# Convolution stage of a mixed convolution and attention block: gram runs joined, subtractions moved and reordered

## What is computed

```python
def _L0_conv_ref(feature, conv_w, conv_b):          # K = 7, PAD = 3
    norm = jnp.sqrt(jnp.sum(feature * feature, axis=1, keepdims=True))
    feat_n = feature / jnp.maximum(norm, EPS)
    feat_pad = jnp.pad(feat_n, ((0, 0), (0, 0), (PAD, PAD), (PAD, PAD)))
    corr = jnp.stack([jnp.sum(feat_pad[:, :, r:h + r, cc:w + cc] * feat_n, axis=1)
                      for r, cc in _offsets()], axis=1)
    x = jnp.concatenate([feature, corr], axis=1)
    return jnp.einsum('bchw,oc->bohw', x, conv_w) + conv_b[None, :, None, None]
...
x = x + _L0_conv_ref(_gn(x), L0_conv_conv_w, L0_conv_conv_b)      # _gn: group norm, 32 groups
t = _to_tokens(x)
t = t + _L1_attn_ref(_ln_t(t), ...)
t = t + _L1_ffn_ref(_ln_t(t), ...)
```

## Time and profile before

| | us |
|---|---|
| median of three runs | 2792.21 (2791.79 to 2792.80) |
| the profiled execution | 2792.42 |
| its span, first to last instruction | 2790.6 |

### The profile page before, as it was taken

How to read it: one execution, slowest core, us unless ns; L and a number is a source line. 1 busy time by engine, 2 the same in 40 slices (tenths; PEclk the granted TensorE clock), 3 DMA queues, 4 the chain that set the end, 5 groups by cost and what they waited for, 6 DMA issues and landing times. The chain is left out here.

```text
span 2790.6 us, 59188 instructions
## 1 busy us (share of the span) xinstructions
PE 2578.2 (92%) x23728; PEld 1255.5 (45%) x23728; DVE 1854.0 (66%) x2383; ACT 1543.3 (55%) x2626; POOL 1420.2 (51%) x1113
## 2 busy tenths in 40 slices
PE   4888568999999999999999999999499999999999
PEld 3555233454544444444544544533144444444444
DVE  6887258888898888888888887785333333333332
ACT  2334035667666676676666666666344444444443
POOL 2333155778778778787778776777210101111010
PEclk8889778999999999999999999999799999999999
DMA  3121232113113112112131121110300101010110
GB/s 139 64 95 56 102 90 69 35 37 106 37 32 102 42 32 99 32 41 90 32 105 36 39 77 45 32 47 2 113 23 23 46 23 45 23 45 23 28 40 23
DMA packets 67442, 151.45 MB, mean 54 GB/s; under 512 B 13313, under 2 KB 17342, under 8 KB 67198
## 3 DMA queue, kind: packets, MB, share of 16 engines
q1 hardware_dynamic: 67198, 148.05, 16.7%
HBM read 59.17 MB, written 37.75 MB: 35 GB/s over the span
## 5 line engine op out<-in xcount | busy, mean ns | idle before, releaser
L1377 POOL TENSOR_TENSOR b_pair<-b_ex 128x512 f32<-128x512 f32 x768 | 975.0, 1296 | 341.7 <-ACT b_ex L1249 341.6
L1249 ACT ACTIVATE b_ex<-b_st 128x512 f32<-128x512 f32 x1536 | 870.1, 598 | 408.1 <-PE b_st L911 372.6
L1084 DVE TENSOR_REDUCE b_mxp<-b_mx 128x4 f32<-128x2048 f32 x384 | 877.8, 2286 | 153.2 <-PE b_mx L927 152.2
L911 PE MATMUL b_st<-b_qst,b_kst 97*128 97x256 f16 (+1 forms) x3072 | 548.5, 277 | 22.0 <-ACT b_ex L1249 8.5
L1633 DVE TENSOR_TENSOR c_gs<-c_g,c_gs 128x512 f16<-128x512 f32 x192 | 132.8, 692 | 482.2 <-ACT c_gs L1706 482.2
L1554 PE MATMUL c_hid<-c_z,c_wi 128*128 128x512 f16 x1728 | 406.3, 381 | 11.3 <-DVE c_z L1626 11.3
L944 PE MATMUL b_pv<-b_ex,b_v 128*32 128x256 f32 x6144 | 411.9, 386 | 1.9 <-ACT b_pvs L1257 1.7
L1569 PE MATMUL c_acc<-c_gs,c_wo 128*128 128x512 f16 x1728 | 404.0, 379 | 0.0
L911 PEld LDWEIGHTS b_st<-b_qst,b_kst 97*128 97x128 f16 (+1 forms) x3072 | 216.0, 97 | 370.6 <-ACT b_ex L1249 201.2
L1702 ACT ACTIVATE c_g<-c_hid,c_bias 128x512 f32<-128x512 f32 x192 | 131.4, 684 | 363.3 <-PE c_hid L1554 363.1
L1554 PEld LDWEIGHTS c_hid<-c_z,c_wi 128*128 128x128 f16 x1728 | 169.5, 98 | 228.3 <-issue 20.2
(11 more groups left out here) (169 smaller groups left out, 2715.5 us busy)
## 6 DMA issues: line engine op xcount, KB each, us to landing
a_x<-in_x SPq DMA_DIRECT2D x8, 1536.0 KB, 9.3
after_conv<-a_x SPq DMA_DIRECT2D x24, 512.0 KB, 2.6
b_xl<-after_conv SPq DMA_DIRECT2D x8, 1536.0 KB, 8.8
b_qst<-b_staged0q SPq DMA_DIRECT2D x192, 64.0 KB, 2.0
b_kst<-b_staged0k SPq DMA_DIRECT2D x192, 64.0 KB, 2.0
b_v<-b_vstaged SPq DMA_DIRECT2D x24, 512.0 KB, 2.9
b_xr<-after_conv SPq DMA_DIRECT2D x8, 1536.0 KB, 6.4
after_attention<-b_xr SPq DMA_DIRECT2D x8, 1536.0 KB, 5.4
```

The source lines that it names most:

```text
L911: last = nc.tensor.matmul(st[n % NST][:, j * QUERIES:(j + 1) * QUERIES], kst[g][0:depth, s, kt * P:(kt + 1) * P], qst[g][0:depth, s, q0:q0 ...
L1084: nc.vector.reduce_max(mxp[x % 2][:, w // 2, :, w % 2], mx[:, :, :], AX_X).then_inc(mx_taken, 1)
L1249: nc.scalar.activation(ex[u % 2][e][s][:, :], st[n % NST][:, :], ACT.Exp, scale=SCALE).then_inc(exp_ready, 1)
L1377: nc.gpsimd.tensor_tensor(pair[u % 2][s][:, :], ex[u % 2][0][s][:, :], ex[u % 2][1][s][:, :], ALU.add).then_inc(pair_ready, 1)
```

## The change

TensorE runs both gram halves in one piece, then sums of squares, then means. VectorE's list is put in another order: masks of half 0, low correlations of image s - 1 (which were the last thing in the step of that image), statistics, masks of half 1, `within_groups`, inverse norms, evictions with unit features. The low halves of the unit features go to GpSimd, at the head of its step, behind a wait for both gram halves of image s. Every instruction that is computed stays the same; only its place changes, and for the low halves the engine.

```diff
                     correlate(0)
+                    correlate(1)
                 if real(s + 1):
                     squared_norms(s + 1)
-                if real(s):
-                    correlate(1)
...
-            def unit_features(i, p, n):
-
-                if n < KC:
-                    dve.wait_ge(clamped, INVERSE * (2 * i + 2))
-                    nc.vector.tensor_tensor(sq[:, n, :], f[p][:, n, :], nrm[:, :], ALU.mult
-                                            ).then_inc(fn_ready, 1)
-                else:
-                    k = n - KC
-                    dve.wait_ge(fn_ready, KC * i + k + 1)
-                    dve.wait_ge(fnhi_ready, KC * i + k + 1)
-                    nc.vector.tensor_tensor(fn[1][:, k, 0:NPIX], sq[:, k, :], fn[0][:, k, 0:NPIX],
-                                            ALU.subtract).then_inc(fnlo_ready, 1)
+            def unit_features(i, p, k):
+                dve.wait_ge(clamped, INVERSE * (2 * i + 2))
+                nc.vector.tensor_tensor(sq[:, k, :], f[p][:, k, :], nrm[:, :], ALU.mult
+                                        ).then_inc(fn_ready, 1)
...
+            def correlation_low(i, p):
+                for c in range(CHUNKS):
+                    at = slice(c * CHUNK, (c + 1) * CHUNK)
+                    dve.wait_ge(chi_ready, CHIGH * i + c + 1)
+                    nc.vector.tensor_tensor(cs[p][CB:CB + BACK, at], corr[c * CB:c * CB + BACK, 0:CHUNK],
+                                            cs[p][0:BACK, at], ALU.subtract).then_inc(clo_ready, 1)
+
             def step(s, p):
                 if real(s):
                     wait(dve, corr_ready, s)
                     keep_shifts(s, 0)
+                if real(s - 1):
+                    correlation_low(s - 1, 1 - p)
                 if real(s + 2):
                     statistics(s + 2)
-                if real(s + 1):
-                    invert_norms(s + 1, 0)
-                    invert_norms(s + 1, 1)
                 if real(s):
                     keep_shifts(s, 1)
                 if real(s + 2):
                     within_groups(s + 2)
+                if real(s + 1):
+                    invert_norms(s + 1, 0)
+                    invert_norms(s + 1, 1)
                 if isinstance(s, int) and s == -1:
                     weights()
                 for n in range(EV):
                     if real(s - 1):
                         evict(s - 1, n)
-                    if real(s + 1):
+                    if real(s + 1) and n < KC:
                         unit_features(s + 1, 1 - p, n)
                 if real(s + 2):
                     features(s + 2, p)
-                if real(s):
-                    for c in range(CHUNKS):
...
         def _(pool):
             def step(s, p):
                 q = 1 - p
+                if real(s + 1):
+                    wait(pool, gram_ready, 2 * s + 2)
+                    for k in range(KC):
+                        pool.wait_ge(fnhi_ready, KC * (s + 1) + k + 1)
+                        nc.gpsimd.tensor_tensor(fn[1][:, k, 0:NPIX], sq[:, k, :], fn[0][:, k, 0:NPIX],
+                                                ALU.subtract).then_inc(fnlo_ready, 1)
```

## The result

The changed kernel takes 2824.37 us (median of four runs, 2823.23 to 2828.01) against 2792.51 us for the kernel before, measured beside it: a ratio of 1.0114 [1.0098, 1.0130] (in brackets here and below: the 95% interval), 31.9 us slower. One of the four runs of the kernel before took 6016.76 us; without it its median is 2792.21 and the difference 32.2. The profiled execution of the changed kernel is the slowest of the four, 2828.01 us, 35.6 above the profiled one of before. Hardly anything of that arises behind the convolution stage: the attention stage's first load is issued at 372.15 us instead of 336.83, 35.3 later.

A forecast was written before the change was run, and what follows sets the result against it. Two chains, TensorE's own and the transfers' 0.7 us behind, bound the convolution's start. Early steps +8.8, steps 1 to 5 +13.4, step 6 +4.0, step 7 +5.3: +31.5 on 2792.21 gives 2823.7 us, range 2807 to 2834.

The forecast's parts named there:

- The transfers' chain: Convolution stage: low correlations behind mask products delay shift transfers, so convolution starts at T+17.6 (T: step's first gram instruction).
- TensorE ready at T+13.6: Steady step: gram in one piece, sums and means done, TensorE could start the convolution 3.4 us earlier than before.
- rival (c): Transfers start after the image load and land sooner; convolution at T+13.6 without cold start, 2779.8 us; chance 0.04.
- The cold start: After the wait for transfers the convolution starts at half the granted clock, costing 2.3 us more per step.
- The prediction's ends, 1.4 and 2.5: Range, in us, for the extra time of a convolution that starts at the lower clock.
- GpSimd in a steady step: Low halves mostly hidden; VectorE and GpSimd holding each other back costs 0.4 us per step, ends 0 and 2.1.
- Rival (b): GpSimd's low halves finish after the select and gram waits for them; 2830 to 2840 us; chance 0.08.
- Before the pipeline is full: Steps -1 and 0: means ahead of VectorE's work +3.5, low halves on GpSimd +2.8, step 0 +2.5; sum +8.8 us.
- high end of 11.2: Upper end, in us, for the early steps: another VectorE operation of 1.2 gets between GpSimd's, twice.
- Step 0's +2.5: Step without convolution: slower low halves on GpSimd +2.8, less 0.3 waited for gram half 1 now.
- (a): Rival: denser TensorE work ahead keeps the clock up over the wait, no cold start; 2807.8 us; chance 0.12.
- (d): Rival: unseen slack from transfers to convolution; gains and losses cancel with the early loss, within 5 us; chance 0.03.

The follow-up runs named there:

- e1: Changed kernel with the low correlations of image s - 1 ahead of the first mask products instead of behind them; 2806.86 us.
- e5: Changed kernel with added matmuls that compute nothing used, behind the sums of squares and behind the means, filling TensorE's wait; 2817.72 us.
- e2: Changed kernel with the low halves of the unit features on VectorE again; 2819.92 us.
- e4: Kernel before with only the two gram runs in one piece ahead of the sums of squares; 2798.97 us.
- e9: e8 with ScalarE's high parts of the features moved behind the squares and the high correlations; 2805.47 us.
- e6: Changed kernel with every second one of the twelve shift transfers issued by ScalarE instead of SyncE; 2807.97 us.
- e8: Kernel before with gram in one piece, transfers shared between SyncE and ScalarE, and statistics one step ahead, before the low correlations; 2786.17 us.
- e3: Changed kernel with the inverse norms ahead of the second mask products and the means' VectorE part, as before the change; 2822.40 us.
- e7: Kernel before with only the low halves of the unit features on GpSimd; 2798.34 us.
- e11: Kernel before with only the low correlations moved behind the next step's first mask products; 2809.57 us.
- e12: e8 with means in their own PSUM bank ahead of the sums of squares, and second mask products ahead of the inverse norms; 2771.61 us.

## Why the prediction was right

It said 2823.7; the median is 2824.4. By its own steps:

**The transfers' chain.** Right in mechanism and place: e1 moves only what the prediction blamed and brings the first transfer and the convolution back by the 1.5 us. The start was T+17.6 in the sum and 17.8 to 18.2 in the profile: in step 5 the first mask product starts 3.88 behind T and not 3.77, and another 0.1 passes up to the first issue; in steps 1, 4 and 6 it is a further 0.2 to 0.4. A reading beside it was wrong and made no difference to the time: the prediction has TensorE ready at T+13.6. The sums of squares were shorter than its 3.8 (1.98 in step 5), but TensorE then waited for the statistics, and the means end at T+14.1 to 15.3 in steps 1 to 5. Against the T+17.0 of before, TensorE's own gain was thus 1.7 to 3.0 us and not 3.4, and rival (c) was priced too low.

**The cold start.** 2.3 in the sum. Measured from convolution to next gram, over the 16.38 of full clock: 2.81, 2.98, 1.47, 2.20, 2.81 in steps 1 to 5, and 2.78 over step 6's 15.05, on average 2.5. e5 shows that it is the clock: filled, 16.39. The prediction's ends, 1.4 and 2.5, were drawn from two convolutions; four of these six lie beyond the upper one.

**GpSimd in a steady step.** 0.4 in the sum, at most 0.15 a step measured (steps 1 to 6 together 219.78, in e2 without GpSimd's part 218.86): a term that was hardly needed, and that made up for most of what the two above lacked. The engines do meet, as forecast. Step 5 of the changed kernel:

```profile
257.58 2.13 POOL L513 TENSOR_TENSOR a_fn<-a_sq,a_fn 128x1024 f16<-128x1024 f32 x1 [11.01 <-ACT a_fn L471]
257.89 2.89 DVE L382 TENSOR_TENSOR a_sq<-a_f,a_nrm 128x1024 f32<-128x1024 f32 x1
```

The unit feature, 1.22 alone, takes 2.89 and ends 1.07 behind the low half's end: it waited out the whole low half. This is the rule of the Trainium skill, "SBUF — State Buffer", section "Who interferes with whom" (a VectorE instruction with two SBUF inputs and a GpSimd instruction that reads SBUF exclude each other), and the trace agrees with it to within 0.2 us. But the next evictions catch up, and the groups of the convolution there start 2.16 to 2.20 us apart: TensorE loses nothing. Rival (b) did not come.

**Before the pipeline is full.** Mis-sized in this execution: +8.8 in the sum, +11.1 measured, close to its high end of 11.2. Step -1 of the changed kernel:

```profile
36.38 3.12 PE L253 MATMUL a_stat<-a_mv,a_gmean 128*128 128x1 f32 x14 [0.78 <-ACT a_nrm L466]
...
47.03 3.49 DVE L382 TENSOR_TENSOR a_sq<-a_f,a_nrm 128x1024 f32<-128x1024 f32 x3
...
49.43 8.14 POOL L513 TENSOR_TENSOR a_fn<-a_sq,a_fn 128x1024 f16<-128x1024 f32 x3 [17.66 <-ACT a_fn L471]
...
52.01 6.11 DVE L420 TENSOR_SCALAR a_f<-a_x,a_gm,a_rs 128x1024 f32<-128x1024 f32 x3
...
57.63 7.59 PE L263 MATMUL a_gram<-a_fn 128*128 128x32 f16 x288 [14.27 <-POOL a_fn L513]
```

Two terms were too small. The means now on the path took 3.12 instead of the 1.69 of the earlier trace rows, so the unit features start 5.0 later and not 3.5. That they take longer is not the change's doing: in e1 and e5, with the same order up to there, they took 1.69 and the first gram started at 55.88 and 56.02, and in e4, with the order of the kernel before, they took 3.12. First e1, then e4:

```profile
36.05 1.69 PE L253 MATMUL a_stat<-a_mv,a_gmean 128*128 128x1 f32 x14 [0.78 <-ACT a_nrm L466]
```

```profile
36.08 3.12 PE L253 MATMUL a_stat<-a_mv,a_gmean 128*128 128x1 f32 x14 [0.78 <-ACT a_nrm L472]
```

And the three low halves took 8.14 instead of 6.31. The first, 3.08, waits for the end of the last unit feature, which the prediction had in its +2.8; each of the two others ends 2.5 us after the one ahead of it, not 2.1, beside the features, which ran undisturbed before and are drawn out themselves, 6.11 against 2.26 where GpSimd is idle. From the start of the unit features to the first gram this is +3.6 where the sum has +2.8; the prediction had such a meeting in its high end only. Step 0's +2.5 was right (+2.43).

**Rivals.** (a), the clock staying up, needs TensorE's wait filled, as e5 shows. (c), transfers that land sooner when they start later: they took 9.56 again (240.44 to 250.00). (d), slack in the chain: there is none, as e1 moves the first transfer and the convolution by the same 1.5 us.

**Luck.** The mechanism was right; that the time is met to within 1 us is partly luck. Step by step the profile adds up to +34.9 where the sum has +31.5: 2.3 too little before the pipeline is full and, in each of six steps, some 0.6 too little for the convolution's start and its clock, against the 0.4 put down for GpSimd that hardly came. The profiled execution, the slowest of the four, is 35.6 above the profiled one of before; it is the median that lies at 31.9.

## What to carry to other kernels

Before shortening one engine's chain, time every other chain that meets it at the same instruction: here the second chain was 0.7 us behind, and that was all there was to win as long as the transfers stayed as they were. An instruction moved in an in-order list takes on the waits of what now stands ahead of it, and puts off what stands behind; four subtractions behind a wait for gram cost 15 us here, and a 2.95 us block in front of the roots 19 us in e9. A wait cost most here in front of the convolution, the longest dense run of matmuls, which then paid for the clock: up to 3.0 us on 13.0, against 1.8 for the sums of squares (3.78 instead of 1.98) where the wait stood before.

## What the runs showed of the hardware that was not expected

- The cold start cost 2.5 us on average (1.5 to 3.0) for a convolution of 13.0 us; the means in the middle of the wait did not keep the clock up (0.50 at the end of the wait in each of steps 1 to 5), the idle-time matmuls of e5 did (1.00).
- Issuing six transfers held ScalarE's list for 4.3 to 4.8 us (e6, e8, e9), about 0.75 each. SyncE alone issues the twelve in 8.21 of the 9.56 us from first issue to first matmul, and on two engines these were 6.2 (e8, step 6), so most of that time was issuing.
- The sums of squares took 1.9 to 2.0 us in six of seven steps of the changed kernel, right behind gram, and 3.78 behind a wait before; the gram, of short matmuls, 3.77 at full clock and 4.00 in step 0, where the granted clock was mostly 0.50.
- In the first 39 us the profile gives a granted clock of 1.00, yet the same means took 1.69 in some executions (the kernel before, e1, e5 and e9) and 3.12 in others (the changed kernel, e2, e3, e4, e6, e7, e8, e11). Both times occur with the same order of instructions up to there, so the order does not set them; what does was not tried and stays open.
- In each kernel with the gram in one piece TensorE stood still inside it in two or three of the steps, 0.9 to 2.5 us each, waiting for nothing that the profile shows (`PE a_gram L263 <- issue` above, twice in the changed kernel); the kernel before, e7 and e11, with two pieces, have none. In the changed kernel the wait for the transfers covers it; in e12 it stands ahead of the two convolutions that no longer wait for transfers. Its cause was not tried.
